# Turning raw rows by products with a diagonal of row factors: one change to a layer norm, attention and feed-forward kernel on one Trainium2 core

## The reference

```python
x = x + attn(layernorm(x))
#   C_q = n @ Wq_d + bq_d (12 columns); C_kv = n @ Wkv_d + bkv_d (4 columns)
#   q = C_q @ W_qk + b_qk (32 heads x 4); scores = q . C_kv / 2; softmax over 2048 keys
#   V = C_kv @ Wv_u + bv_u (32 heads x 32); out = (attn @ V) @ Wo + bo
x = x + ffn(layernorm(x))
#   n @ W.T + bias + the sum of 8 LoRA updates of rank 16
layernorm(x) = (x - mean) / sqrt(var + 1e-5)
```

## Time and profile before

| | us |
|---|---|
| median of 3 runs | 2121.74 |
| lowest and highest | 2119.95 and 2122.32 |
| the profiled execution | 2122.61 |
| its span, first to last instruction | 2120.8 |

### The profile page before, as it was taken

The page is one execution under the profiler, slowest core; times in us unless marked ns, Lnnn a source line. Parts: engine busy times, 40 slices in busy tenths (PEclk is TensorE's granted clock), DMA queues, the critical chain, the costliest instruction groups (busy, mean ns, idle before and its releaser), DMA issues. The chain is left out here.

```text
span 2120.8 us, 35990 instructions
## 1 busy us (share of the span) xinstructions
PE 1958.8 (92%) x15023; PEld 710.0 (33%) x15023; DVE 504.6 (24%) x1307; ACT 1993.5 (94%) x2193; POOL 180.0 (8%) x100
## 2 busy tenths in 40 slices
PE   4757899899999999999999999999999999999999
PEld 3411222233333333333333333333333333333337
DVE  8732343212111111212111111212111111212115
ACT  6968999999999999999999999999999999999970
POOL 1210001000010001100010001100020001100021
PEclk8989999999999999999999999999999999999999
DMA  7541201000010000100010000100010000100010
GB/s 240 184 122 38 84 13 35 5 15 20 18 45 6 25 13 25 35 15 15 24 45 5 25 13 25 35 15 13 25 45 5 22 16 25 35 15 13 25 40 40
DMA packets 45661, 77.42 MB, mean 37 GB/s; under 512 B 15870, under 2 KB 29750, under 8 KB 45498
## 3 DMA queue, kind: packets, MB, share of 16 engines
q1 hardware_dynamic: 45498, 75.11, 10.8%
HBM read 51.23 MB, written 23.86 MB: 35 GB/s over the span
## 5 line engine op out<-in xcount | busy, mean ns | idle before, releaser
L573 ACT ACTIVATE probs<-ps 128x1024 f32<-128x1024 f32 x2048 | 1900.1, 1030 | 34.3 <-PE ps L783 23.8
L794 PE MATMUL ps<-probs,c_wide 128*32 128x512 f32 x8192 | 989.8, 601 | 0.0
L783 PE MATMUL ps<-q_in,key_t 27*128 27x512 bf16 x4096 | 405.1, 386 | 102.9 <-ACT probs L573 91.4
L840 PE MATMUL ps<-w_eff,xn_t 128*128 128x512 f32 x1344 | 394.6, 418 | 0.0
L794 PEld LDWEIGHTS ps<-probs,c_wide 128*32 128x32 f32 x8192 | 212.7, 108 | 426.6 <-issue 221.6
L783 PEld LDWEIGHTS ps<-q_in,key_t 27*128 27x128 bf16 x4096 | 103.0, 91 | 734.7 <-ACT probs L573 714.9
L1263 DVE SCALAR_TENSOR_TENSOR y<-ps,nw,y 128x512 f32<-128x512 f32 x64 | 48.0, 751 | 977.5 <-PE ps L840 967.7
L840 PEld LDWEIGHTS ps<-w_eff,xn_t 128*128 128x128 f32 x1344 | 228.2, 188 | 102.2 <-issue 69.8
L481 POOL TENSOR_TENSOR y<-y,ffn_bias 128x1024 f32<-128x1024 f32 x32 | 76.4, 2387 | 1355.3 <-DVEq L1284 1355.3
L476 POOL TENSOR_TENSOR y<-y,attn_bias 128x1024 f32<-128x1024 f32 x32 | 75.5, 2381 | 481.2 <-DMA y<-in_L_attn_x_dram 481.0
L1247 DVE TENSOR_TENSOR y<-ps,y 128x512 f32<-128x512 f32 x64 | 44.2, 690 | 137.5 <-PE ps L817 137.1
(11 more groups left out here) (136 smaller groups left out, 593.8 us busy)
## 6 DMA issues: line engine op xcount, KB each, us to landing
y<-in_L_attn_x_dram SPq DMA_DIRECT2D x48, 512.0 KB, 4.2
out_dram<-y SPq DMA_DIRECT2D x32, 512.0 KB, 2.7
area<-in_L_attn_x_dram SPq DMA_DIRECT2D x16, 512.0 KB, 4.9
q_in<-q_parts SPq DMA_DIRECT2D x256, 27.0 KB
q_parts<-q_parts_sb SPq DMA_DIRECT2D x48, 128.0 KB, 2.2
y<-in_L_attn_Wo_dram SPq DMA_DIRECT2D x1, 2048.0 KB, 8.5
xn<-in_L_attn_Wo_dram SPq DMA_DIRECT2D x1, 2048.0 KB, 13.5
y<-in_L_ffn_W_dram SPq DMA_DIRECT2D x1, 2048.0 KB, 7.7
```

What stands on the lines that cost most here:

```text
L573: nc.scalar.activation(probs[:, (c * STEPS + step) % PROBS, bass.ts(pair, 2 * N)], ps[:, 2 * (i % SCORE_SLOTS):2 * (i % SCORE_SLOTS) + 2, ...
L783: last = nc.tensor.matmul(ps[:, at, :], key_t[TILE * h:TILE * h + KEYS, bass.ts(b * KT + kt, P)], q_in[TILE * h:TILE * h + KEYS, g % 2, :] ...
L794: last = nc.tensor.matmul(ps[32 * h:32 * h + 32, SUMS, :], c_wide[:, b * KT + kt, at:at + 32], probs[:, (c * STEPS + step) % PROBS, bass.t ...
L840: last = nc.tensor.matmul(ps[:, SHARED, :], xn_t[:, t % 2, a, kb, :], w_eff[:, b, kb, bass.ts(half, N)], start=(kb + i == 0), stop=(kb == ...
```

## The change

1. ACT no longer normalises. The mean leaves through the weights: `w_down` gets its column mean subtracted, from a product with ones (`first_weights`) and two DVE operations. The row factor of chunks 0 and 1 is applied after the down product: PE spreads it over a bank (`spread_r`), ACT moves it (`move_r`), DVE multiplies (`scale_parts`). For chunks 2 to 7 the transposes become fp32 products of the raw tile with a diagonal matrix of the row factors (`turn_x`).
2. POOL works out the factors and the diagonals (`deviations_x`). DVE only measures. POOL's loop is written out, with the query splits of chunk c-3 behind the factors of chunk c.
3. Four buffers hold raw chunks in place of two; loads wait for a chunk to be turned and measured.
4. The end of the stage: `largest(0)` and `bounds(0)` move into the middle of chunks 6 and 7, in bank 6; `split_shift` takes the maximum straight from the bank and negates it later; the last chunk's maximum goes ahead of its cast, and `q_abs` goes first in the last `move_products`. PE's third step of attention waits for `bound_read`.
5. SP: the group-1 queries are loaded right behind those of group 0; the value, LoRA and Wo loads come ahead of the last `store_q` and shift stores.

The core of the diff:

```diff
-        x_tiles = [y, xt_b]
+        x_tiles = [y, xn, xt_b, xn_b]
+        diags = [diag, o_q]
+        SPREAD = 2
+            def load_tiles(c):
+                if c >= RING:
+                    sp.wait_ge(t_ready, START + (c - RING + 1) * KB)
+                    sp.wait_ge(x_measured, c - RING + 1)
+                for t in range(TT):
+                    sp.dma_start(x_tiles[c % RING][:, t, :], x_t[c * TT + t]).then_inc(x_in[c % RING][t], 16)
...
             load_q(0, 0, 0, q_loaded[0])
+            load_q(0, 1, 1, q_loaded[1])
             store_shifts(0, 1, CB)
+            sp.wait_ge(t_ready, START + CHUNKS * KB)
+            sp.wait_ge(x_measured, CHUNKS)
+            sp.dma_start(wv_in, wv_u).then_inc(lora_in, 16)
+            for a in range(KB):
+                sp.dma_start(lora_b_sb[:, a], lora_b[:, a * P:(a + 1) * P, :].rearrange("n o r -> o n r")
+                             ).then_inc(lora_in, 16)
+            for half in range(2):
+                sp.dma_start(w_stage[half][:, :, :].rearrange("p t (a n) -> p (t a) n", n=N),
+                             wo[:, half * N:(half + 1) * N].rearrange("(a p) n -> p a n", p=P)).then_inc(stage_in[half], 16)
             for c in (CHUNKS - 2, CHUNKS - 1):
                 store_q(c, c % 2)
...
+            def deviations_x(c):
+                slot = c % 2
+                v, a, r = (x_r[:, slot, i, :] for i in range(3))
+                pool.wait_ge(x_measured, c + 1)
+                pool.tensor_scalar(v, x_mv[:, slot, :, 1], EPS, None, ALU.add).then_inc(p_r, 1)
...
+                pool.tensor_scalar(r.bitcast(I32), v.bitcast(I32), -0.5, float(0x5F3759DF), ALU.mult, ALU.add).then_inc(p_r, 1)
...
+                for i in range(3):
+                    pool.tensor_tensor(a, r, r, ALU.mult).then_inc(p_r, 1)
...
+                    pool.tensor_tensor(a, a, v, ALU.mult).then_inc(p_r, 1)
...
+                    pool.tensor_scalar(a, a, -0.5, 1.5, ALU.mult, ALU.add).then_inc(p_r, 1)
...
+                    pool.tensor_tensor(r, a, r, ALU.mult).then_inc(p_r, 1)
...
+                if c >= SPREAD + 2:
+                    pool.wait_ge(t_ready, START + (c - 1) * KB)
+                elif c >= 2:
+                    pool.wait_ge(r_ps, c - 1)
+                pool.tensor_tensor(diags[c % 2][:, :, :], ident[:, :].unsqueeze(1).to_broadcast([P, TT, P]),
+                                   r.unsqueeze(2).to_broadcast([P, TT, P]), ALU.mult).then_inc(diag_ready, 1)
...
+            for c in range(CHUNKS):
+                deviations_x(c)
+                if c >= 3:
+                    split_q(c - 3)
...
-            def normalise(c, slot, t):
-                nc.scalar.activation(xn_tiles[slot][:, t, :], x_tiles[slot][:, t, :], ACT.Identity,
-                                     bias=nw[:, slot, 2, t:t + 1], scale=nw[:, slot, 3, t:t + 1]).then_inc(xn_ready, 1)
...
+            def move_r(c):
+                act.wait_ge(r_ps, c + 1)
+                act.wait_ge(part_ready, START + c)
+                nc.scalar.activation(o_sb[:, :], ps[:, 5, :], ACT.Copy).then_inc(r_moved, 1)
...
+            def first_weights():
...
+                last = nc.tensor.matmul(ps[:, 7, 32:32 + KB * 32], ones[:, :], w_down[:, :, :].rearrange("p k n -> p (k n)"),
+                                        start=True, stop=True)
+            def turn_x(c, kb):
...
+                    last = nc.tensor.matmul(ps[:, kb % 4, bass.ts(t, P)], x_tiles[c % RING][:, t, bass.ts(kb, P)],
+                                            diags[c % 2][:, t, :], start=True, stop=True)
...
+            def spread_r(c):
+                pe.wait_ge(diag_ready, c + 1)
+                pe.wait_ge(lat_ready, START + c)
+                nc.tensor.matmul(ps[:, 5, :], ones[:, :], diags[c % 2][:, :, :].rearrange("p t n -> p (t n)"), start=True, stop=True
+                                 ).then_inc(r_ps, 1)
...
+                                if first and step == BEHIND:
+                                    pe.wait_ge(bound_read, 2)
...
-                ch.then(nc.vector.tensor_scalar(shift, ps[0:rows, bank, :], -1.0, None, ALU.mult))
-                if smallest is not None:
-                    ch.then(nc.vector.tensor_reduce(smallest, shift, AX.X, ALU.min))
+                if largest is not None:
+                    ch.then(nc.vector.tensor_reduce(largest, ps[0:rows, bank, :], AX.X, ALU.max))
                 if then:
                     then()
+                ch.then(nc.vector.tensor_scalar(shift, ps[0:rows, bank, :], -1.0, None, ALU.mult))
+                dve.sem_inc(bound_read, 1)
...
+            def scale_parts(c):
+                dve.wait_ge(spread_ps, START + c)
+                dve.wait_ge(q_ps, START + c)
+                dve.wait_ge(down_done, (c + 2) * KB)
+                dve.wait_ge(r_moved, c + 1)
+                nc.vector.tensor_tensor(down_part[:, :], ps[:, 4, :], o_sb[:, :], ALU.mult).then_inc(part_ready, 1)
...
+            statistics(1)
+            statistics(2)
+            for c in range(1, CHUNKS):
+                if c - 1 < SPREAD:
+                    scale_parts(c - 1)
+                if c == CHUNKS - 2:
+                    weigh(0, 6)
+                if 2 <= c < CHUNKS - 1:
+                    split_latents(c - 2, c % 2)
+                if c == CHUNKS - 2:
+                    split_latents(c - 1, 1 - c % 2)
+                if c == CB + 1:
+                    largest(0)
+                if c + 2 < CHUNKS:
+                    statistics(c + 2)
             dve.wait_ge(bound_ps, 1)
```

More of the change, by code:

```diff
@@ L206, in build_block @@
         bound_ps = sem("bound_ps")
+        bound_read = sem("bound_read")
         shift_split = sem("shift_split")
@@ L322, in _ @@
             sp.dma_start(lora_a_sb[:, :], lora_a.rearrange("n r d -> (n r) d")).then_inc(lora_in, 16)
[L325 to L328 removed]
+            load_tiles(2)
+            load_tiles(3)
             def store_q(c, slot):
@@ L416, in beside_attention @@
                 for g in range(G4):
-                    if not (first and g == 0):
-                        sp.wait_ge(s_ready, PAIRS * (c * G4 + g))
+                    if first and g == 0:
+                        continue
+                    sp.wait_ge(s_ready, PAIRS * (c * G4 + g))
                     if g < G4 - 1:
@@ L472, in _ @@
+            for c in range(CHUNKS):
+                deviations_x(c)
+                if c >= 3:
+                    split_q(c - 3)
+            for c in range(CHUNKS - 3, CHUNKS):
+                split_q(c)
             pool.wait_ge(prep_ok, PREP_W)
@@ L605, in down @@
                     pe.wait_ge(part_ready, START + c)
+                if c == 0 and four == 0:
+                    pe.wait_ge(down_ok, 4)
                 for i in range(4):
@@ L636, in bounds, with stage1 @@
                 pe.wait_ge(bound_w_ready, b + 1)
+                pe.wait_ge(q_read, START + (b + 1) * CB)
                 for j in range(CB):
-                    last = nc.tensor.matmul(ps[32 * j:32 * j + H, b, :], bound_w[:, b, :], q_abs[:, b * CB + j, :],
+                    last = nc.tensor.matmul(ps[32 * j:32 * j + H, bank, :], bound_w[:, b, :], q_abs[:, b * CB + j, :],
                                             start=True, stop=True)
                 last.then_inc(bound_ps, 1)
-            def stage1(c, slot, first=False, beside=None):
-                pe.wait_ge(xn_ready, (c + 1) * TT)
+            def stage1(c):
@@ L645, in stage1 @@
                 for kb in range(KB):
-                    turn_x(c, slot, kb)
-                    if kb == 1 and not first:
-                        down(c - 1, 1)
+                    turn_x(c, kb)
+                    if kb == 3 and c == 0:
+                        first_weights()
+                    if kb == 0 and c and c - 1 < SPREAD:
+                        spread_r(c - 1)
+                    if kb == 1 and c:
+                        down(c - 1, 1)
+                    if kb == 2 and c == CHUNKS - 2:
+                        pe.wait_ge(caug_ready, START + c - 1)
+                        largest(0, 6)
@@ L649, in stage1 @@
+                    if kb == 2 and c == CHUNKS - 1:
+                        pe.wait_ge(caug_ready, START + c - 1)
+                        bounds(0, 6)
+                    if kb == 3 and c:
+                        sum_parts(c - 1)
                     if kb == 5:
                         down(c, 0)
-                    if kb == 3 and not first:
-                        if beside is bounds:
-                            pe.wait_ge(bound_w_ready, 1)
-                        sum_parts(c - 1)
-                    if kb == 6 and not first:
-                        use_latents(c - 1, 1 - slot)
@@ L657, in stage1 @@
-                if beside:
-                    beside(0)
-            stage1(0, 0, True)
-            for i in range(CHUNKS // 2 - 2):
-                for half in range(2):
-                    stage1(i * 2 + half + 1, 1 - half)
```

(21 more changed lines are left out.)

224 lines of the change are left out of this document (119 added, 105 removed).

## The result

Eight runs of the changed kernel have a median of 2114.2 us (2113.42 to 2116.28), beside 2121.4 us for eight of the kernel before (2119.35 to 2124.8). The ratio is 0.9968, with a 95% interval of 0.9959 to 0.9978: about 6.8 us faster (4.7 to 8.7). The profiled execution took 2114.35 us, its span is 2112.6 us. Against 2122.61 and 2120.8 before, that is 8.2 us of span, and it is this difference that the rows explain.

A forecast was written before the change was run, and what follows sets the result against it. ACT's exponentials were taken to bound the kernel, so only an earlier first exponential and fewer idle places could gain: 3.1 + 2.3 + 4.2 = 9.6 off 2,122.6, and 0.9 lower against the median, 2,112 us; range 2,104 to 2,124.

The forecast's parts named there:

- `statistics(1)` starts: Start of the stage, DVE: measuring chunk 1 starts at 18.9, a microsecond later than before.
- `scale_parts(0)` starts: Start of the stage, DVE: chunk 0's scaling comes only after `statistics(2)` ends at 29.6 and takes 0.7.
- chunk 1 turned: Start of the stage, PE: chunk 1 ends at 38.5, bounds 35.6 and 40.6, where it was 43.54.
- six chunks on PE: Chunks 2 to 7: 11.19 us each, PE-bound, plus `spread_r(1)` and the moved `bounds` and `largest`, 69.2 in all.
- turn to `tight`, gain: End of the stage: verdict `tight` 12.95 us after the last turn, before 15.2, a gain of 2.3.
- `tight` to first score, gain: From the verdict to PE's first score matmul: 5.0 us as before, no gain.
- idle places of ACT in attention, gain: Change to group 1: its early load removes ACT's idle 2.32 and 1.89 us, a gain of 4.2.
- (c): Start of the stage, PE: reaches `sum_parts(0)` by 29.8 at the latest, waits until 30.5, ends chunk 1 at 38.5.
- Rival B: Stage ahead of attention: POOL is the bound at 12.1 a chunk, 2,117 us, over 2,140 at twice the price; chance 0.12.
- Rival A: PE's products: weight loads are not hidden, a pass is 0.216, 2,153 us; decides from 0.134 per pass; chance 0.11.
- Rival C: Verdict to first score: transfers beside the verdict delay PE, the gap grows by 8.5, 2,120 us; chance 0.10.
- Rival D: Early stretch: higher clock throughout and the weights there at 11.5, 2.9 + 1.6 less, 2,107.5 us; chance 0.12.

The follow-up runs named there:

- after_order: The changed kernel with `scale_parts(0)` ahead of `statistics(2)` on DVE, products kept: 2113.98 us, ratio 0.996.
- after_late: The changed kernel with the value, LoRA and Wo loads put back behind the last stores and SP's branch: 2114.89 us, ratio 0.9967.
- after_turns: The changed kernel with transposes in place of the products in chunks 2 to 7, their row factor left out of the result: 2103.5 us, ratio 0.9917.
- after_half: The changed kernel with each product's diagonal cut to its first 64 columns, half of each turned block not written: one run, 2113.22 us.
- spread7_order: The changed kernel with the first seven chunks scaled after the down product and `scale_parts(0)` ahead of `statistics(2)` on DVE: 2101.5 us, ratio 0.9904.
- after_pad64: The changed kernel with 64 unread semaphore increments on PE ahead of its first work: 2119.09 us, ratio 0.9994.
- before_pad32: The kernel before with 32 unread semaphore increments on PE at its start: 2120.79 us, ratio 0.9998.

## Why the prediction was right in its total and wrong in two of its terms

Forecast 2,112 us, measured 2114.2. The total is right in part by luck: two errors of 3.7 us cancelled. Taken step by step on the profiled executions:

| step | forecast | measured |
|---|---|---|
| `statistics(1)` starts | 18.9 | 18.95 |
| `scale_parts(0)` starts | 29.8 (ready 30.5) | 31.44 |
| chunk 1 turned | 38.5 | 39.06 |
| six chunks on PE | 69.2 | 72.4 |
| last turn, gain against before | 107.7, +3.1 | 111.42, -0.6 |
| turn to `tight`, gain | 12.95, +2.3 | 12.48, +2.7 |
| `tight` to first score, gain | 5.0, 0 | 1.35, +3.7 |
| first exponential | near 126 | 125.97 |
| idle places of ACT in attention, gain | +4.2 | +3.3 |
| behind the last exponential | 0 | -1.0 |
| sum | 9.6 | 8.1 |

**What held.** ACT's bound changed into one of PE. The start of the stage came to within 0.6 us, with PE waiting for DVE at the first `sum_parts`, as (c) had it. The wait was longer than forecast since PE got there sooner (26.5) and DVE waited 1.17 for a tile of chunk 2; PE then ran at half the clock until 35.8. The end of the stage, with `bounds(0)` and `largest(0)` moved, was worth what was worked out in this execution. In others it was worth less: from the last turn to `tight` it took 13.40 in after_order and 14.66 in after_late, where PE's granted clock fell some 3.5 and 5.5 us sooner (estimates from windows of 1 us). POOL was hidden. Its chain shows in its own timeline in the changed kernel:

```profile
62.36 0.27 POOL L485 TENSOR_SCALAR x_r<-x_mv 128x4 f32<-128x4 f32 x1
...
67.14 0.20 POOL L496 TENSOR_TENSOR x_r<-x_r 128x4 f32<-128x4 f32 x1
67.42 1.04 POOL L502 TENSOR_TENSOR o_q<-ident,x_r 128x512 f32<-128x512 f32 x1
```

A small operation is mostly 0.20, one every 0.28, and 14 of them take 4.0 us in the first chunks but 5.1 in chunks 4 to 6 (62.36 to 67.42), where 3.5 had been taken; the diagonal is 1.04 where 1.2 had been taken. From one chunk to the next POOL needs 9.2 and not 8.2. Rival B (POOL sets the pace) didn't come, but after_turns shows that it stood right behind PE. Rival A (the loads not hidden) didn't come either: a pass is 0.112, far from the 0.134 where it would decide. The Trainium skill's page TensorE: Matmul & The Clock Gate, section The mechanism, says in its list that a weight load overlaps a matmul only where their row groups differ, though the same section, above that list, also names the background weight buffer as a case. Here loads and matmuls both use all 128 rows, the load's record is 192 ns, and passes follow at 112: in this kernel they overlap, against the sentence that the prediction drew on. Rival C fell with after_late, and SP's queue was through 36.9 us after the last turn, where 33 had been taken, 9 us ahead of the load of group 2 at 157.57. Rival D (the early stretch at the higher clock throughout, the weights there at 11.5) didn't come: DVE's first step of preparation started at 13.18, and PE's clock was low behind its wait.

**The first wrong term: six chunks on PE.** It was forecast at 69.2 and measured 72.4. A pass is 0.1117 and not 0.109, which is 0.17 us per chunk. The rest is the switching: wherever the kind of matmul changes, the first record comes about 0.1 late, and a chunk of products interleaved with `down`, `sum_parts` and `use_latents` has four such places, which the sum of pieces, each read from before, holds only in part. Together a chunk is 11.69 and not 11.19, and the chunks with `spread_r`, the moved `largest` and the moved `bounds` (12.54, 11.90 and 12.87) add the rest. The step said that every 0.01 us on a pass costs 3.8 us. The cause that it gave for the pitch was wrong as well: it took the stream for what sets it and the load for hidden, and in after_half half the stream leaves the pitch at 0.112. This error in the cause cost next to nothing here, where a stream of 128 columns and the pitch are nearly the same. It would cost much to someone who shortens the stream.

The same term holds the larger miss. Since the products were costed as a swap at an even pace, 11.2 for 11.19, it was not asked what the same change would give without them. It is 14.2 us at the last turn (after_turns), and in a form that computes the reference, with the order on DVE changed too, 12.7 us of the total (spread7_order beside the change: 2101.5 and 2114.2, from two comparisons with the same kernel before). The Trainium skill's Perfetto Trace Analysis, section Transposes, advises against a matmul where a transpose will do. The runs agree, and give the price: a transposed block costs one pass of 0.109, a product two of 0.112.

**The second wrong term: `tight` to the first score.** It was carried over at 5.0 as a fixed cost of the branch. It is fixed only for one place in the instruction stream: in 14 kernels it is either 1.3 to 1.4 or 4.6 to 5.0 us, and a packet of instructions moves in it when it is long, and none when it is short. The change has 198 more matmuls on PE (15,221 beside 15,023), and landed on the short side by luck. The two errors, -3.7 and +3.7, cancelled, and so the first exponential came near 126 as forecast.

**A third one, smaller.** The load of group 1 was worth its 4.2 us in the idle places that it was meant for. But 0.9 of it went again elsewhere: in both kernels PE is at the lower clock (1.2 GHz) until about 138, though the first exponential starts 5.8 us apart. It is 0.50 in the window from 121 to 138. The first idle place grew from 1.65 to 2.35, and a new one of 1.39 stands where the clock has just risen; the one of 2.15 at 189 shrank to 0.95. Together that is the 0.9 between forecast and measured.

**What stays open.** The gap's worth in time isn't settled. Of the 4.9 us that after_pad64 lost, 1.96 lie ahead of the last turn and come from the increments themselves, which leaves about 3 for the opened gap; closing it in the kernel before gave 0.4 and 2.3 us, both with intervals of 2 to 3 us either way, and in the first of the two part of it was handed back to the queue of group 1. Hence by the runs alone the change's 6.8 us are 3.6 of early load and 3.2 of everything else. How those 3.2 divide between the end of the stage, which gained 2.7 in the profiled execution and less in others, and the gap rests on single profiled executions. When the clock rises is open too: at 138 in both kernels, whose attention starts 5.8 us apart, and that is 6.6 us behind the first exponential in one and 12.1 in the other; in after_order it rose at about 134.6 and in before_pad32 at about 136.1, 7.2 and 7.4 behind (estimates from windows of 1 us).

## What to carry to other kernels

Where work is moved from a saturated engine to one with room, add up that engine's new queue first, and then ask what the same edit would be with a cheaper form of the moved work: here the row factor applied behind the projection (per chunk one product to spread it, one move and one multiplication of 512 columns) beats the one folded into the turn (64 passes in place of 32) by 12.7 us, once the order on DVE lets it. A wait that is removed at the start of a pipeline is worth only what the next dependence leaves: the same one-line reordering gave 4.4 us or nothing to be told from noise. And the gap behind this branch changes with where the code lies, so don't credit it to a design before some instructions that do nothing have been put ahead of it.

## What the runs showed of the hardware that was not expected

- PE's gap behind a branch that passes over a long body has two sizes, 1.3 to 1.4 and 4.6 to 5.0 us from the same verdict to the same matmul. Shifting the code by 32, 64 or 128 instructions switches it. In all 4 kernels with the long one a 16 KB packet of the instruction queue moves in it, in none of the 10 with the short one.
- An increment of a semaphore on PE costs about 0.15 us. 64 of them ahead of the first work put off the first transpose by 6.3 us, to 11.97; 128 of them put the first matmul of the kernel before at 20.49. The 0.15 is an estimate from these two.
- Back-to-back fp32 passes with a 128x128 weight load each follow at 0.112 us, with 128 moving columns or with 64 (one run with 64).
- Small POOL operations of 128x4 take 0.20 us, but up to 0.73 where they run beside certain DVE operations: one of 0.73 at 54.31 runs beside DVE's L1165 (54.24 to 54.99), and one of 0.57 at 55.86 beside L1169 (55.63 to 56.38). I take it for contention between the two; no run tested that.
- The same instructions at the end of stage 1 took 12.48, 13.40 and 14.66 us from the last turn to the verdict (the change, after_order, after_late), the longer the sooner PE's granted clock fell to 0.50 (at about 121, 117.5 and 115.5, estimates from windows of 1 us).
